# Two transformer layers on one core: the queries' place in the plan, and the rows of their leading products

## The reference, cut to what matters

```
x0 = x0 + g * mha(mod(ln(x0)))            # self attention within the half; the same for x1
x1 = x1 + g * mha(mod(ln(x1)))
xm, ym = mod(ln(x0)), mod(ln(x1))
x = x + concat(g * attend(q(xm), k(ym), v(ym)), g * attend(q(ym), k(xm), v(xm)))   # across the halves
x = x + g * mlp(mod(ln(x)))               # gelu, hidden width 1024
```

```
x = ln(x + mha(x, x, x, mask))            # "sa"
x = ln(x + mha(x, memory, memory))        # "ca"
x = ln(x + relu(x @ w1 + b1) @ w2 + b2)
```

## Time and profile before

| | |
|---|---|
| median of 3 runs | 2372.28 us (2369.52 to 2376.15) |
| the profiled execution's own time | 2370.26 us |
| its span, first to last instruction | 2368.4 us |
| mean granted TensorE clock | 0.914 |
| PE busy | 2053.3 us (87%) |
| DVE busy | 1566.2 us (66%) |
| ACT busy | 1286.5 us (54%) |
| POOL busy | 472.8 us (20%) |
| DMA, share of 16 engines | 23.1% |

### The profile page before, as it was taken

The page is one execution under the profiler, slowest core; times in us unless marked ns, Lnnn a source line. Parts: engine busy times, 40 slices in busy tenths (PEclk is TensorE's granted clock), DMA queues, the critical chain, the costliest instruction groups (busy, mean ns, idle before and its releaser), DMA issues.

```text
span 2368.4 us, 33832 instructions
## 1 busy us (share of the span) xinstructions
PE 2053.3 (87%) x12890; PEld 794.1 (34%) x12890; DVE 1566.2 (66%) x2867; ACT 1286.5 (54%) x2406; POOL 472.8 (20%) x464
## 2 busy tenths in 40 slices
PE   4689998898888898997987696999799999999975
PEld 2323223222232342532522251232244334434424
DVE  3488897786667657465465545796566996796703
ACT  1036675565445665754764372478424775585660
POOL 0022424332131202022021312110213002102100
PEclk8769999999799999998998897799879999999988
DMA  6624134522043202035014513020201102000000
GB/s 150 121 64 95 64 87 106 102 70 64 13 105 70 66 6 62 21 79 99 4 45 90 105 34 74 20 44 6 66 4 39 33 11 52 12 6 13 12 15 11
DMA packets 97305, 126.66 MB, mean 53 GB/s; under 512 B 25293, under 2 KB 81982, under 8 KB 92014
## 3 DMA queue, kind: packets, MB, share of 16 engines
q1 hardware_dynamic: 97134, 124.42, 23.1%
HBM read 89.95 MB, written 24.74 MB: 48 GB/s over the span
## 4 chain that ended last, share of the span: by engine, by line
PE 61%; DVE 13%; ACT 7%; DMA 7%; POOL 5%; issue 5%; SPq 3%; POOLq 0%; ACTq 0%; DVEq 0%
PE ps L1368 17%; PE ps L1322 15%; PE ps L1343 12%; DVE mx L1605 7%; PE ps L1474 5%; PE ps L1427 3%; SPq L1134 3%; PE ps L1463 3%; ACT PT L1536 3%; DMA QS<-scr 2%; PE ps L1451 2%; PE ps L1439 2%; DMA scr<-S 2%; DVE st L1628 1%; ACT big L1578 1%
## 5 line engine op out<-in xcount | busy, mean ns | idle before, releaser
L1605 DVE TENSOR_REDUCE mx<-ps 128x1 f32<-128x512 f32 x2048 | 1283.4, 683 | 337.9 <-PE ps L1343 335.0
L1536 ACT ACTIVATE PT<-ps 128x512 f32<-128x512 f32 (+1 forms) x2112 | 1099.9, 602 | 727.6 <-PE ps L1322 721.7
L1343 PE MATMUL ps<-KS,QS 49*128 49x512 bf16 x2048 | 553.6, 412 | 185.5 <-DVE mx L1605 87.6
L1322 PE MATMUL ps<-QS,KS 51*128 51x512 bf16 (+3 forms) x4224 | 627.6, 394 | 5.4 <-DMA QS<-mr 5.0
L1368 PE MATMUL ps<-PT,Vt 128*32 128x512 f32 (+1 forms) x4224 | 590.5, 631 | 0.0
L1343 PEld LDWEIGHTS ps<-KS,QS 49*128 49x128 bf16 x2048 | 149.0, 96 | 795.8 <-DVE mx L1605 515.6
L1322 PEld LDWEIGHTS ps<-QS,KS 51*128 51x128 bf16 (+3 forms) x4224 | 211.8, 98 | 274.6 <-ACT PT L1536 84.9
L1844 POOL CAST nm<-nm 128x16 bf16<-128x16 f32 x64 | 12.7, 198 | 718.1 <-DVE nm L1618 718.1
L1368 PEld LDWEIGHTS ps<-PT,Vt 128*32 128x32 f32 (+1 forms) x4224 | 85.0, 109 | 154.0 <-issue 150.1
L1463 PE MATMUL ps<-XT,big 128*128 128x256 f32 x512 | 125.6, 396 | 2.9 <-ACT big L1578 1.5
L1427 PE MATMUL ps<-XT,wA 128*128 128x512 f32 (+1 forms) x216 | 109.4, 633 | 11.3 <-DMA wA<-in_L_xattn_ca_qw 5.2
(11 more groups left out here) (106 smaller groups left out, 1122.9 us busy)
## 6 DMA issues: line engine op xcount, KB each, us to landing
scr<-S SPq DMA_DIRECT2D x28, 768.0 KB, 3.6
big<-in_mask_1x1xSxS_ik SPq DMA_DIRECT2D x16, 1024.0 KB, 5.2
QS<-scr SPq DMA_DIRECT2D x32, 384.0 KB, 9.5
KS<-scr SPq DMA_DIRECT2D x24, 384.0 KB, 8.3
QS<-scr SPq DMA_DIRECT2D x32, 256.0 KB, 7.5
ON<-Oe SPq DMA_DIRECT2D x256, 32.0 KB
OD<-scr_r SPq DMA_DIRECT2D x32, 256.0 KB
KS<-scr SPq DMA_DIRECT2D x24, 256.0 KB, 7.2
```

Of the source, the lines that this page charges most:

```text
L1322: z = eng.matmul(ps[0:w, it.bank[j], :], KS[lo:hi, part, pr, col:col + w], QS[lo:hi, part, u.qs, pr, :], start=part == 0, stop=part == 1 a ...
L1343: return eng.matmul(mbank(it)[:, 0:w], QS[lo:lo + MR, 0, u.qs, pr, 128 * it.tq:128 * it.tq + 128], KS[lo:lo + MR, 0, pr, it.lo:it.hi], sta ...
L1536: eng.activation(PT[0:w, it.pt * 4 + 2 * it.pp + j, :], ps[0:w, it.bank[j], :], ACT.Exp, scale=0.25).then_inc(S["exp_done"], 1)
L1605: eng.tensor_reduce(out=mx[:, u.b, c, it.i:it.i + 1], in_=mbank(it)[:, 0:it.hi - it.lo], axis=AX.X, op=ALU.max).then_inc(S["max_done"], 1)
```

## The change

There are four parts. The query chains are posted when the chunk's x is ready, with a due time but no longer when the slot is free; `to_dram` writes them to one of two new DRAM buffers, one for each slot, and where the slot is taken, `to_rows` is held in `held_rows` until the chunk in the slot has ended, and comes one entry of `later` after that. The six DMAs of the rows are issued in another order, the four of part 0 first, which raise the old semaphore; the two of part 1 raise a new one (q_lo..., k_lo...), for which only the steps wait. `Track.next` leaves out a chain whose first entry waits for something not yet ended. The loads of `crs_start`, of the biases and of layer 1's weights (`slow`) come six steps later, or ahead of the next output product, normalisation or mlp entry.

```diff
-        scr = [dram(f"scr{i}", [2 * 3 * P * CH], BF16) for i in range(4)]
+        scr = [dram(f"scr{i}", [2 * 3 * P * CH], BF16) for i in range(6)]
...
-                later.extend([[SPLIT[0], flush_ends], [SPLIT[1], lambda: to_dram(it)], [SPLIT[2], lambda: to_rows(it)]])
+                later.extend([[SPLIT[0], flush_ends], [SPLIT[1], lambda: to_dram(it)]])
...
-                of.k = it.k = n["scr_use"] % 4
-                n["scr_use"] += 1
+                of.k = it.k = 4 + slot if q else n["scr_use"] % 4
+                n["scr_use"] += not q
                 it.scr_free = mark.get(("scr_free", it.k))
                 dma(it, "scr_out", 1)
                 of.out = it.landed
+                if not q or not taken[slot]:
+                    later.append([SPLIT[2], lambda: to_rows(of)])
+                else:
+                    assert slot not in held_rows
+                    held_rows[slot] = lambda: to_rows(of)
...
-                dma(it, name, 6)
-                mark["scr_free", it.k] = (name, it.landed)
-                if not q:
+                it.lo_was, it.lo_sem = n[name.replace("in", "lo")], name.replace("in", "lo")
+                mark["scr_free", it.k] = (it.lo_sem, up(it.lo_sem, 32))
+                dma(it, name, 4)
+                if q:
+                    taken[slot] = True
+                else:
                     mark["k", name] = (name, it.landed)
+                    mark["klo", name] = mark["scr_free", it.k]
...
+            def next(self, force):
+                known = ended | ({c[3] for c in ends_track.queue} | {ends_track.key} if force else set())
+                return min((i for i, c in enumerate(self.queue) if not isinstance(c[2][0][0], str) or c[2][0][0] in known),
+                           key=lambda i: (self.queue[i][:2], i), default=None)
...
+            for f in slow:
+                f[0] -= 1
+            while slow and slow[0][0] <= 0:
+                slow.pop(0)[1]()
...
                     if hg == 3:
+                        taken[qs] = False
+                        if qs in held_rows:
+                            later.append([1, held_rows.pop(qs)])
                         ph.post(c, qs)
...
-                work.post(8, q_l0(2, 0, 0), 0)
...
-                work.post(12, q_l0(3, 1, 0) + [(0, lambda: l0_weights("crs"))], 0)
...
         work.post(8, kv_l0(2, 0))
         work.post(8, kv_l0(3, 0))
+        work.post(8, q_l0(2, 0, 0), 2)
+        work.post(8, q_l0(3, 1, 0) + [(0, lambda: l0_weights("crs"))], 3)
...
-            work.post(17, out_l0(3, 0) + [(0, crs_start)])
+            work.post(17, out_l0(3, 0) + [(0, lambda: slow.append([6, crs_start]))])
             work.post(20, kv_l0(3, 1, 1))
-            work.post(24, kv_l0(2, 1))
+            work.post(22, kv_l0(2, 1))
+            work.post(24, q_l0(0, 0, 1))
+            work.post(28, q_l0(1, 1, 1), 0)
...
                 if c == 2:
-                    work.post(24, q_l0(0, 0, 1), 0)
...
                 elif c == 3:
-                    work.post(28, q_l0(1, 1, 1), 0)
                     work.post(29, out_l0(3, 1))
                     work.post(31, mlp0(3))
                     work.post(32, sa_kv(now()))
+                    work.post(32, x_q(2, 0, "sa"))
+                    work.post(36, x_q(3, 1, "sa"))
...
                 elif c == 0:
-                    work.post(32, x_q(2, 0, "sa"), 0)
                     work.post(33, out_l0(0, 1))
                     work.post(36, mlp0(0))
+                    work.post(40, x_q(0, 0, "sa"))
                 else:
-                    work.post(36, x_q(3, 1, "sa"), 0)
-                    work.post(36, out_l0(1, 1) + [(0, l1_out_start)], 0)
+                    work.post(36, out_l0(1, 1) + [(0, lambda: slow.append([6, l1_out_start]))], 0)
                     work.post(44, ctx_kv(1, 512, 4, now()))
                     work.post(44, ctx_kv(2, 512, 4, now()))
-                    work.post(48, mlp0(1) + [(0, l1_mlp_start)])
+                    work.post(44, [("sa2", lambda: None)] + x_q(2, 1, "ca"), 0)
+                    work.post(48, x_q(1, 0, "sa"))
+                    work.post(52, [("sa3", lambda: None)] + x_q(3, 1, "ca"))
+                    work.post(56, [("sa0", lambda: None)] + x_q(0, 0, "ca"))
+                    work.post(60, [("sa1", lambda: None)] + x_q(1, 1, "ca"))
+                    work.post(47, mlp0(1) + [(0, lambda: slow.append([6, l1_mlp_start]))])
...
-                    for j in range(2):
-                        for part, lo, t, k in ((0, 0, 0 if it.q else 2, 1), (0, 16, 0 if it.q else 1, 2), (1, 0, 0, 3)):
+                    for part, lo, t, k in ((0, 0, 0 if it.q else 2, 1), (0, 16, 0 if it.q else 1, 2), (1, 0, 0, 3)):
+                        if part == 1:
+                            q.wait_ge(S[it.lo_sem], it.lo_was)
+                        for j in range(2):
...
+                    q.wait_ge(S[f"q_lo{u.qs}"], it.q_lo)
+                    for name, v in u.kdep + u.klo:
```

More of the change, by code:

```diff
@@ L332, in __init__ @@
                 self.kdep = [mark[k] for k in ph.kdep(c) if k in mark]
+                self.klo = [mark["klo", k] for _, k in ph.kdep(c) if ("klo", k) in mark]
                 self.vdep = max([mark["v", k] for k in ph.vdep(c) if ("v", k) in mark], default=0)
@@ L501, in do_out @@
         def do_out(c, gate, gbi):
+            flush_slow()
             at["out"] = 0
@@ L634, in step @@
                             self.key = None
-                        if not self.queue:
+                        i = self.next(force)
+                        if i is None:
                             return
-                        self.due, _, chain, self.key = self.queue.pop(
-                            min(range(len(self.queue)), key=lambda i: (self.queue[i][:2], i)))
+                        self.due, _, chain, self.key = self.queue.pop(i)
                         self.cur.extend(chain)
@@ L657, in step, with flush_slow @@
                         return
+        taken, held_rows = [False, False], {}
+        slow = []
+        def flush_slow():
+            while slow:
+                slow.pop(0)[1]()
         ended = set()
@@ L941, in xattn_kernel @@
         bg_until(999)
+        flush_slow()
+        flush_later()
+        assert not held_rows
+        kept_taken = list(taken)
         for f in side:
@@ L985, in post @@
                 if c == 2:
-                    work.post(24, q_l0(0, 0, 1), 0)
-                    work.post(25, out_l0(2, 1) + [(0, lambda: gate_bias(2, I["L0_xattn_mlp_fc2_b"]))])
+                    work.post(25, out_l0(2, 1) + [(0, lambda: slow.append([6, lambda: gate_bias(2, I["L0_xattn_mlp_fc2_b"])]))])
                     work.post(28, mlp0(2))
                 elif c == 3:
-                    work.post(28, q_l0(1, 1, 1), 0)
                     work.post(29, out_l0(3, 1))
@@ L1010, in post_sa @@
             def post_sa(c, qs):
-                if c == 2:
-                    work.post(40, x_q(0, 0, "sa"), 0)
-                    end_l1(44, 2, "sa")
-                elif c == 3:
-                    work.post(44, [("sa2", lambda: None)] + x_q(2, 1, "ca"), 0)
-                    end_l1(48, 3, "sa")
-                elif c == 0:
-                    work.post(48, x_q(1, 0, "sa"), 0)
-                    end_l1(52, 0, "sa")
-                else:
-                    work.post(56, [("sa0", lambda: None)] + x_q(0, 0, "ca"), 0)
-                    end_l1(60, 1, "sa")
+                end_l1({2: 44, 3: 48, 0: 52, 1: 60}[c], c, "sa")
             def post_ca(c, qs):
-                if c == 2:
-                    work.post(52, [("sa3", lambda: None)] + x_q(3, 1, "ca"), 0)
-                elif c == 3:
-                    work.post(60, [("sa1", lambda: None)] + x_q(1, 1, "ca"), 0)
                 end_l1(99, c, "ca")
@@ L1061, in load_mask @@
             it.c, it.slot = c, c % 2
-            it.copied, it.ones, it.q_in = n["mk_copy"], n["ones_set"], n[f"q_in{c % 2}"]
+            it.copied, it.ones = n["mk_copy"], n["ones_set"]
+            it.q_in, it.q_lo = n[f"q_in{c % 2}"], n[f"q_lo{c % 2}"]
             take_m(it)
@@ L1124, in xattn_kernel @@
         unit0[0] = kept_unit0
+        assert not (held_rows or slow or later)
+        taken[:] = kept_taken
         general()
@@ L1353, in pe_part @@
                     q.wait_ge(S["mk_step"], it.mask)
-                    for name, v in u.kdep:
+                    q.wait_ge(S[f"q_lo{u.qs}"], it.q_lo)
+                    for name, v in u.kdep + u.klo:
                         q.wait_ge(S[name], v)
@@ L1816, in dve_part @@
                     q.wait_ge(S[f"q_in{it.slot}"], it.q_in)
+                    q.wait_ge(S[f"q_lo{it.slot}"], it.q_lo)
                     for lo in (0, 64):
```

11 lines of the change are left out of this document (6 added, 5 removed), and 5 rows, old and new, of the table S.

## The result

| | before | after |
|---|---|---|
| median (range) of 5 runs each, on the same chip | 2372.28 us (2365.04 to 2380.10) | 2353.86 us (2352.01 to 2357.81) |
| the profiled execution's own time | 2370.26 us | 2357.39 us |
| its span | 2368.4 us | 2355.5 us |
| mean granted clock | 0.914 | 0.921 |

The ratio is 0.9925, with a 95% interval of 0.9897 to 0.9953. The change made the kernel 18 us faster, where 79 were forecast (2295, range 2262 to 2336): outside the range, on the right side of zero.

A forecast was written before the change was run, and what follows sets the result against it. It took TensorE to bound the kernel, with its waits for query rows second. 60.5 + 13.5 + 15 - 10 = 79 us off 2370.3, plus 2.0 for the median and 2 for norms, gave 2295; range 2262 to 2336.

The forecast's parts named there:

- the four waits: Layer 1, at 1257, 1352, 1464 and 1707 us: TensorE's waits for query rows all go, 60.5 us gained.
- Norms, 2 us: Norms, planned by counts of steps, have less time to be ready once the stalls go: 2 us lost.
- Rival 2: In sa, norms, QS<-mr and weights each come late and the clock falls as before: 36 us gained, 2336; chance 0.18.
- Moved chains, 0: Query chains moved to earlier units in layer 0, ca and from sa cost the same at both places: 0.
- the bound of 8: Two sa chains (chunks 3 and 0) moved into layer 0: taken as 0, between -8 and +8 us.
- QS<-mr, 10 us in sa, covered in layer 0: Next unit's QS<-mr stands behind released rows: 5.0 us lost at each of two sa chunk ends, out of 0 to 30.
- rows of part 0 first: Maxima wait for four DMAs, not six: 4.5 us gained at 569 us, 721 us and the head, 13.5 in all.
- rival 3: Chains leave the queue no earlier; part 0 first alone acts at seven places: 31 us gained, 2341; chance 0.05.
- Slow loads, 0: Late loads save SP time, such as 3.2 us for a bias, ahead of rows no longer late: 0.
- The clock, 15: Half-clock stretches after the six stalls: 15 us come back if the clock stays up, out of 0 to 29.
- rival 1: All throttled time is paid by half, and half of it goes with the stalls: 2262; chance 0.13.
- Weights, 0: 8 us new wait for sa_qw near 1030 us against 8 of the old 9.6 gone: 0, from -8 to +8.

The follow-up runs named there:

- e1: Changed kernel, but held rows of queries issued behind the ended chunk's two norm loads, not ahead: 2323.81 us.
- e3: Changed kernel with layer 0's early queries, main attention and across the halves, posted again only when their slot falls free: 2331.81 us.
- e4: Changed kernel with both held rows behind the norm's loads and layer 0's queries posted when their slot falls free: 2299.36 us.
- e13: Kernel before with the new order of rows and the late loads, without early queries: 2317.26 us.
- e10: Changed kernel with the old order of rows and the loads at once, leaving early queries alone: 2398.58 us.
- e2: Changed kernel with the queries of chunks 2 and 3 of layer 0's first attention posted again when their slot falls free: 2340.27 us.
- e8: Changed kernel with the first two query chains of layer 0 begun 14 and 10 steps later: 2358.54 us.
- e5: Changed kernel with the six row DMAs in the old order and the maxima waiting for all six: 2384.6 us.
- e9: Kernel before with only the new order of rows and their own semaphores: 2335.29 us.
- e6: Changed kernel with the loads of weights, biases and scales at once again, not six steps later: 2371.25 us.
- e12: Kernel before with only the loads of weights, biases and scales six steps later: 2362.24 us.
- e11: e4, with more layer-1 query and context-key rows also waiting behind a norm under way, and sa's weights asked for earlier: 2288.21 us.

## Why the prediction was wrong

An account by place, worked out from the first exponential of the unit in each profile: how much later (+) or earlier (-) than before the unit begins, in us.

| at the start of unit | after | e1 | e3 | e4 | e13 |
|---|---|---|---|---|---|
| 0 | -2.4 | -6.6 | -3.5 | -7.0 | -7.4 |
| 9 (layer 0, chunk 2) | +12.5 | +7.4 | -3.6 | -7.1 | -7.5 |
| 19 (across the halves) | +7.2 | +1.8 | -11.4 | -14.0 | -14.8 |
| 26 | +15.0 | +10.4 | -10.3 | -12.3 | -12.8 |
| 32 (layer 1) | +19.4 | +15.0 | -5.8 | -7.4 | -20.7 |
| 45 (ca 2) | -15.8 | -35.1 | -41.0 | -56.4 | -51.9 |
| 63 (last) | -15.4 | -44.0 | -38.9 | -68.9 | -58.9 |

The first row is the head, which differs by some us between executions. The change enters layer 1 19 us *later* than before, and wins 35 there, where the four waits alone were 60.5. What came in layer 1 beside them: 38 us of waits of the output product, of which at most 5 were there before, while the 5.2 us for ca_qw went. That leaves 33, so the clock and the moved chains together gave some 2 us there.

**The step that failed** is the pricing of the early queries, in three terms. The sum had 60.5 us for the four waits and little against it; alone, early queries made the kernel 24 us slower (e10).
- *Norms, 2 us.* "The stalls were also time in which GpSimd and the DMAs caught up" saw that norms would have less time, but not that the rows themselves would delay them. What the sum lacked is the count of what else is issued at the release of the slot: the end of a chunk's last unit releases both the rows and the norm, and the norm's first DMA had 1.5 MB in front of it. It measured 34.8 us in the waits (5.2 before) and 30 us in e1. The 9.5 us at 1071 us in the trace of before would have priced it. Rival 2, "another wait takes the place", held this with 2336 and was the nearest in mechanism; it put the sizes at some us each, and not at 8 more per chunk.
- *Moved chains, 0.* "The same price at both places" is refuted: units 1 and 2 went from 31.5 and 22.4 us to 40.4 and 35.2, which is 21.7 more, and the units that lost the chains (4 and 8) gave back 5.8 and 2.7. Across the halves unit 19 took 12.1 more and units 20 and 24 gave 3.9 and 3.8. e2 and e3 priced it at 14 and 8 us. The windows of the first two chains, units 1 and 2 of the kernel after, then the same before (from:to, length, busy by engine, clock, DMA share, GB/s):

```profile
175.50:215.90 40.40, 38.20 (x213) 13.08 (x209) 27.64 (x57) 21.38 (x40) 14.97 (x14) 0.92 0.50 102
215.90:251.00 35.10, 29.72 (x181) 9.11 (x177) 26.16 (x49) 19.07 (x37) 18.19 (x15) 0.90 0.35 106
```

```profile
178.00:209.40 31.40, 30.48 (x197) 10.92 (x193) 23.70 (x42) 19.08 (x37) 11.97 (x10) 1.00 0.50 108
209.40:231.80 22.40, 21.61 (x165) 6.31 (x162) 21.26 (x37) 16.93 (x34) 5.65 (x6) 1.00 0.50 94
```

  Unit 2 before was full: VectorE busy 21.26 of 22.40, TensorE 21.61. A chain put there finds no idle time, and it costs more than its own work: with it, VectorE was busy only 26.16 of 35.10. Unit 4 gave back only 5.8 of 32.3. Why the old places gave back so little isn't settled; a neighbouring chain isn't the reason (e8). In layer 1, units 26 to 31 took 12.8 us more with the chains of chunks 3 and 0 of sa in them (e4 from -12.3 to -7.4, e13 from -12.8 to -20.7). Unit 32, which lost one, took 5.0 us less. What the other gave back is mixed with the waits, so whether the bound of 8 held isn't known.
- *QS<-mr, 10 us in sa, covered in layer 0.* It is the other way round: none in sa, four new ones of 3.0 to 4.6 us in layer 0. "Seven steps" were counted and not timed: a step of layer 0 is 1.3 us (21.0 for 16), so seven are 9 us, below the 11.8 of the rows. In the change the norm adds to it. SP stood on the landing of scr_r<-dd before it issued QS<-mr, 4 us ahead of the step at 298.72:

```profile
279.12 2.70 SPq L1169 DMA_DIRECT2D QS<-scr  x6
...
282.33 0.43 SPq L1169 DMA_DIRECT2D scr_r<-dd  x1
293.29 1.35 SPq L1169 DMA_DIRECT2D OD<-scr_r  x2
294.75 1.13 SPq L1169 DMA_DIRECT2D QS<-mr  x2
```

  e1 took that away (QS<-mr at 284.20, right behind the rows), and this wait stayed, 3.9 us: then the rows' bytes alone are enough. The term was near in sum (18.9 less the old 5.0, where 10 were forecast), its place was wrong. e3 removes half of it, and of the 9.5 us left, e13 without early queries has 9.2.

**Right in mechanism, wrong in size: rows of part 0 first.** 13.5 us forecast, 31 (e5) and 39 (e9) measured. Per place the forecast had 4.5, by the nearest row; the runs show 5.6 to 6.0, since the part-0 rows of 256 KB landed in 4.8 us when issued first and not in 5.9. More weighty is the number of places: taken alone it acts at the seven that rival 3 counted, 7 x 5.8 = 41. That this meets the 39 is partly chance. By unit, the five waits at 569, 1257, 1352, 1464 and 1707 us gave 29, the head only 2 by the first unit, and that at 721 nothing, as QS<-mr took its place; the rest came elsewhere, mainly 5.5 us in units 27 and 28. In the change, with the four layer-1 waits gone, it is still worth 31; 21 of them are read from the traces of e5 and after: the head's wait 18.8 and 12.4 us, that at 569 us 9.9 and 4.2, and QS<-mr 27.8 and 18.9. (The profiled execution of e5 took 2400.5 us, the longest of 14, so these may be high.) The other 10 were not followed.

**Slow loads, 0.** 17 us (e6) and 12 (e12). The sum looked only at the bias of the earlier trace rows. In the change 8.6 of the 17 come from the large loads ahead of ca's weights. Alone, on the kernel before, the late loads also cut the wait at 1257 us, from 19.8 to 12.5 us.

**The clock, 15.** The granted clock rose from 0.914 to 0.921. Time at the half clock, by 2 x (1 - clock) x span, was 407 us before and 372 after. Of the four stretches, that at 1352 us is gone, and that at 1257 gave way to one of 10 us around the output product's wait at 1251. The long ones at the start of ca became shorter, and stayed. After, in windows:

```profile
1437.00:1442.00 5.00, 3.20 (x25) 0.97 (x21) 4.93 (x16) 2.87 (x6) 1.68 (x4) 1.00 0.00 0
...
1442.00:1465.80 23.80, 21.98 (x78) 5.21 (x79) 18.67 (x35) 4.82 (x9) 4.69 (x2) 0.50 0.06 18
1691.40:1722.10 30.70, 28.54 (x99) 7.07 (x100) 23.97 (x44) 6.50 (x12) 4.69 (x2) 0.50 0.02 5
```

  From the output product at 1427 to the fall at 1442 TensorE had no idle time above 1.4 us, but just ahead of the fall VectorE was the bound (4.93 of 5.00) and left TensorE busy 3.20 of 5.00. A wait of 7.7 us stands ahead of 1427, so the new waits could be the cause. e11 speaks against it: no wait of the output product at these two chunk ends is above 3.7 us there, and TensorE still ran 34.0 and 30.7 us at 0.50 behind them (from 1391.8 and 1630.7 us). So the stalls alone don't bring the half clock. VectorE stands at 78% in both, as in the earlier trace rows. The premise of rival 1, that half of the throttled time goes with the stalls, failed; its price for that time was not tested by itself. Nor does a run isolate the 15 us of the forecast; by the account of layer 1 above, most of it didn't come.

**Weights, 0.** sa_qw made TensorE wait 6.4 us at 1053 (8 forecast), and ca_qw no longer does: right.

The sign that the prediction named for being wrong, TensorE's idle time moving to the norms, showed for more than half of the 60.5 us. The chances put 0.93 on faster, which it was, but by luck: the part that was to bring the gain lost 24 us, and two parts that were to bring 13.5 and 0 carried it. The range failed because the norms' 2 and the moved chains' 0 stood there by argument and not by a row of the very place. Its own bounds were also tighter than the terms: clock 0, QS<-mr 30, weights 8 and part 0 first 0, all taken together, give 2295 + 15 + 20 + 8 + 13.5 = 2351.5, and not 2318.

## What to carry to other kernels

When a transfer is moved to the release of a buffer, list everything else that the same event releases, in queue order and in bytes. Here the large transfer was best issued behind the small one that stood on the next chain, and a queue of its own for the small one gave only 8 of the 30 us. Taking a wait away by doing work earlier pays only where the earlier place has slack, so read the busy shares of that very unit; here both small parts, kept without the large one, were faster than the whole. Where pieces of a transfer have different first readers, issue the first-read half first with a semaphore of its own.

## What the runs showed of the hardware

- A 32 KB DMA from SBUF to DRAM landed in 1.5 us where nothing large was ahead (median of the 16 before, one of which had large ones ahead), and in 9.0 us where 12 of the 16 were issued behind 1.5 MB of reads on the same queue; from ScalarE's queue still in 6.6 us.
- With six DMAs of 1.5 MB in flight the order of issue decides the landing: the 256 KB pieces took 4.8 us issued ahead and 7.5 mixed, while the 384 KB pieces, now last, took 8.4 in place of 9.5.
- TensorE fell to 0.50 of its clock (1.2 of 2.4 GHz) at 1442 us of the change with no idle time above 1.4 us since 1427, in a stretch that VectorE bounded; in the 5 us ahead it was busy 3.20, at 1.00. In e11, with waits of 3.7 us at most at these chunk ends, stretches of 34.0 and 30.7 us at 0.50 remained.
